# A graph-attention walk over sorted edges: the exponent's bound moved into the target table, and a quarter of each step's product moved from VectorE to ScalarE

## The reference

```python
feat = (h @ W).reshape(N, H, D)
el = einsum('nhd,hd->nh', feat, attn_l); er = einsum('nhd,hd->nh', feat, attn_r)
e = leaky_relu(el[src] + er[dst], 0.2)
emax = segment_max(e, dst); ex = exp(e - emax[dst])
denom = segment_sum(ex, dst); alpha = ex / denom[dst]
rst = segment_sum(feat[src] * alpha[..., None], dst)
out = h + elu(rst + bias)
```

## Time and profile before

| | us |
|---|---|
| median of 3 runs | 1996.78 (1994.44 to 1999.62) |
| the profiled execution, its own time | 1998.07 |
| its span from first to last instruction | 1996.4 |
| DVE busy in the span | 1503.7 (75%), 4295 instructions |
| POOL busy | 1325.6 (66%), 1235 instructions |
| PE busy | 1659.0 (83%) |
| ACT busy | 854.8 (43%) |

### The profile page before, as it was taken

The page is one execution under the profiler, slowest core; times in us unless marked ns, Lnnn a source line. Parts: engine busy times, 40 slices in busy tenths (PEclk is TensorE's granted clock), DMA queues, the critical chain, the costliest instruction groups (busy, mean ns, idle before and its releaser), DMA issues.

```text
span 1996.4 us, 48372 instructions
## 1 busy us (share of the span) xinstructions
PE 1659.0 (83%) x11492; PEld 1334.3 (67%) x11493; DVE 1503.7 (75%) x4295; ACT 854.8 (43%) x2066; POOL 1325.6 (66%) x1235
## 2 busy tenths in 40 slices
PE   7767777777787788888887675947999999999996
PEld 5545455555556677666765454936888998988885
DVE  6667677878777888888889888988666666666663
ACT  4633344444433444444444443583444434344442
POOL 2077777777777777677767774404777777777774
PEclk8979999999999999999999988557999999999998
DMA  7745556565534554444444553851333333333342
GB/s 218 231 122 144 161 148 172 151 175 159 135 110 113 141 141 128 132 138 135 127 119 131 155 193 106 301 196 35 54 51 46 51 47 52 49 47 51 46 51 28
DMA packets 150531, 238.93 MB, mean 120 GB/s; under 512 B 27984, under 2 KB 116168, under 8 KB 149192
## 3 DMA queue, kind: packets, MB, share of 16 engines
q0 software_dynamic: 62784, 134.26, 30.2%
q1 hardware_dynamic: 85944, 103.15, 15.6%
q10 hardware_dynamic: 1744, 0.85, 0.2%
HBM read 181.73 MB, written 56.44 MB: 119 GB/s over the span
## 4 chain that ended last, share of the span: by engine, by line
PE 31%; issue 19%; DVE 18%; POOL 18%; DVEq 6%; DMA 6%; POOLq 1%; ACT 0%; SPq 0%; ACTq 0%
POOL w_s L805 16%; PE bank L2233 13%; PE bank L2253 13%; DVE w_s L1501 5%; DMA w_s<-table,w_s 3%; DVEq L1436 3%; DMA out<-mid_g,acc 2%; PE bank L2219 1%; DVE w_s L1491 1%; PE bank L2046 1%; DVE w_s L1487 1%; DVE w_s L1484 1%; DMA w_s<-in_x 1%; DVE acc L1512 1%; DVE acc L1664 1%
## 5 line engine op out<-in xcount | busy, mean ns | idle before, releaser
L805 POOL DMA_INDIRECT w_s<-table,w_s x784 | 840.3, 1072 | 281.8 <-issue 235.3
L2046 PE MATMUL bank<-w_s 128*128 128x260 f32 x1952 | 513.3, 409 | 93.7 <-DVE w_s L1501 91.9
L2046 PEld LDWEIGHTS bank<-w_s 128*128 128x128 f32 x1952 | 375.0, 199 | 194.5 <-DVE w_s L1501 118.7
L1501 DVE SCALAR_TENSOR_TENSOR w_s<-w_s 128x256 f32<-128x256 f32 x976 | 347.7, 417 | 0.0
L1001 ACT COPY w_s<-bank 128x512 bf16<-128x512 bf16 x244 | 143.6, 588 | 409.0 <-PE bank L2026 314.3
L2233 PE MATMUL bank<-acc,w_s 128*128 128x256 f16 x2688 | 303.8, 273 | 0.0
L2253 PE MATMUL bank<-w_s,acc 128*128 x2688 | 302.6, 273 | 1.0 <-DVE acc L1914 1.0
L2253 PEld LDWEIGHTS bank<-w_s,acc 128*128 128x128 f16 x2688 | 262.7, 98 | 32.0 <-issue 1.3
L2233 PEld LDWEIGHTS bank<-acc,w_s 128*128 x2688 | 263.4, 98 | 30.8 <-issue 0.2
L862 POOL DMA_INDIRECT out<-mid_g,acc x112 | 196.4, 1753 | 80.7 <-POOL acc L857 47.0
L1468 DVE SCALAR_TENSOR_TENSOR w_s<-w_s,iota 128x512 bf16<-128x512 f32 x244 | 182.9, 749 | 6.7 <-issue 1.4
(11 more groups left out here) (301 smaller groups left out, 2226.5 us busy)
## 6 DMA issues: line engine op xcount, KB each, us to landing
stage<-in_L_ffn_W SPq DMA_DIRECT2D x32, 512.0 KB, 3.3
w_s<-table,w_s POOLq DMA_INDIRECT x784
w_s<-in_x SPq DMA_DIRECT2D x48, 256.0 KB, 4.2
w_s<-xT_d SPq DMA_DIRECT2D x96, 128.0 KB
w_park<-low_g SPq DMA_DIRECT2D x18, 512.0 KB
w_s<-w_park SPq DMA_DIRECT2D x9, 1024.0 KB, 9.2
xn_d<-acc SPq DMA_DIRECT2D x7, 896.0 KB, 4.7
table<-w_s SPq DMA_DIRECT2D x24, 260.0 KB, 3.6
```

Of the source, the lines that this page charges most:

```text
L805: pool.indirect_dma_start(out=ring[:, u, k, :], out_offset=None, in_=table[:, :], in_offset=bass.IndirectOffsetOnAxis(ap=ids[:, h, at + u, ...
L1501: last = dve.scalar_tensor_tensor(m[:, e:e + GH, 0:GD], rows[:, e:e + GH, 0:GD], 1.0, m[:, e:e + GH, GD:HC].to_broadcast([P, GH, GD]), ALU ...
L2046: last = pe.matmul(bank[2 + k.at % 2][:, 0:ROW], hot32[:, k.at % 4, s, :], msg[:, k.at % 2, s, :], start=s == 0, stop=s == SUB - 1)
```

## The change

It has two parts.

1. The number to subtract is stored in the table without a cap: `cap` is the leaky ReLU of the largest el of all heads (one number), and `most` in the table becomes most - cap. In the step, n = 3 becomes (most + cap) - logit, and the exponential is taken with a scale of -1. The minimum with 0 (n = 4) goes. Counts on `logit_turn` go from 5 to 4 a step. `goal` has two buffers. Three small DVE operations are added ahead of the walk.
2. The product of the last lot of 128 edges of each step is made by ACT, behind the exponential: four activations of 128x64 (one per head) with function Copy and the weight as a per-partition scale. DVE makes three pieces, and waits ahead of the third for ACT's (`part_ready`). ACT loads one register value per slot for it.

Two waits are also merged: the loads of the router's weights count on `mix_in` (9 loads in place of 7), and those who waited for 7 wait for 9.

```diff
@@ act_slot, act_weight
                 if (j + 1).live():
-                    act_weight(j + 1)
+                    slot = act.value_load(walk_i[0:1, bass.ds(j.n + 4, 1), 3:4].rearrange("p a b -> p (a b)"), min_val=0, max_val=RING - 1)
+                    act_weight(j + 1, slot)
...
-            def act_weight(k):
-                act.wait_ge(logit_turn, 5 * k.n + 5)
+            def act_weight(k, slot):
+                act.wait_ge(logit_turn, 4 * k.n + 4)
                 if k.past(2):
                     act.wait_ge(sum_ready, k.n - 1)
-                act.activation(weights(k), logit[:, k.at % 2, :, :].rearrange("p s h -> p (s h)"), ACT.Exp).then_inc(weight_ready, 1)
+                act.activation(weights(k), logit[:, k.at % 2, :, :].rearrange("p s h -> p (s h)"), ACT.Exp,
+                               scale=-1.0).then_inc(weight_ready, 1)
+                act.wait_ge(weight_ready, k.n + 1)
+                m, rows = heads_at(msg[:, k.at % 2, :, :]), ring_heads(slot)
+                for e in range((SUB - 1) * GH, SUB * GH):
+                    last = act.activation(m[:, e, 0:GD], rows[:, e, 0:GD], ACT.Copy, scale=m[:, e, GD:HC])
+                last.then_inc(part_ready, 1)
@@ DVE, ahead of the walk
+            cap = spread[:, 1:2]
...
                     lambda: dve.scalar_tensor_tensor(most, most, SLOPE, most, ALU.mult, ALU.max),
+                    lambda: dve.tensor_reduce(cap, top_n[:, 0:GH], AX.X, ALU.max),
+                    lambda: dve.scalar_tensor_tensor(cap, cap, SLOPE, cap, ALU.mult, ALU.max),
+                    lambda: dve.tensor_scalar(most, most, cap, None, ALU.subtract),
@@ dve_slot
                 if scores:
                     dve_logit(j + 1, group1, slot1, 3)
-                    dve_logit(j + 1, group1, slot1, 4)
@@ dve_logit
-                elif n == 3:
-                    last = dve.scalar_tensor_tensor(lg, lg, 1.0, most, ALU.mult, ALU.subtract)
                 else:
-                    last = dve.scalar_tensor_tensor(lg, lg, 0.0, lg, ALU.min, ALU.min)
+                    last = dve.scalar_tensor_tensor(lg, most, cap, lg, ALU.add, ALU.subtract)
@@ dve_msg
-                for e in range(0, SUB * GH, GH):
+                for e in range(0, (SUB - 1) * GH, GH):
+                    if e == (SUB - 2) * GH:
+                        dve.wait_ge(part_ready, k.n + 1)
                     last = dve.scalar_tensor_tensor(m[:, e:e + GH, 0:GD], rows[:, e:e + GH, 0:GD], 1.0,
                                                     m[:, e:e + GH, GD:HC].to_broadcast([P, GH, GD]), ALU.mult, ALU.mult)
@@ POOL ahead of the walk; PE ahead of the first keys
-            pool.wait_ge(mix_in, 7 * 16)
+            pool.wait_ge(mix_in, 9 * 16)
@@ PE ahead of the walk
-            pe.wait_ge(top_turn, 15)
+            pe.wait_ge(top_turn, 18)
```

More of the change, by code:

```diff
@@ L262, in build @@
         ids = walk([P, 2, LIST * RING, SUB], I32)
-        goal = walk([P, SUB, 2 * GH])
+        goal = walk([P, 2, SUB, 2 * GH])
         iota_i = walk([P, 256], I32)
@@ L465, in build @@
         target_ready, logit_turn, weight_ready = sem("target_ready"), sem("logit_turn"), sem("weight_ready")
-        msg_ready, sum_ready, acc_done = sem("msg_ready"), sem("sum_ready"), sem("acc_done")
+        msg_ready, part_ready, sum_ready, acc_done = sem("msg_ready"), sem("part_ready"), sem("sum_ready"), sem("acc_done")
         xa_in, kv_made, keys_ready, k_parts, keys_mapped, kv_summed = (
@@ L475, in build @@
         base_read, mid_out = sem("base_read"), sem("mid_out")
-        route_in, blank_turn = sem("route_in"), sem("blank_turn")
+        blank_turn = sem("blank_turn")
         park_in, park_high, park_low, park_out = sem("park_in"), sem("park_high"), sem("park_low"), sem("park_out")
@@ L572, in load_mix @@
                 elif n == 7:
-                    sp.dma_start(wr_s[:, :, :], wr.rearrange("(k p) n -> p k n", p=P)).then_inc(route_in, 16)
+                    sp.dma_start(wr_s[:, :, :], wr.rearrange("(k p) n -> p k n", p=P)).then_inc(mix_in, 16)
                 else:
-                    sp.dma_start(br_b[:, :], br.rearrange("(a n) -> a n", a=1).to_broadcast([P, X])).then_inc(route_in, 16)
+                    sp.dma_start(br_b[:, :], br.rearrange("(a n) -> a n", a=1).to_broadcast([P, X])).then_inc(mix_in, 16)
             load_x(0, 0)
@@ L1477, in dve_logit @@
                 lg = logit[:, k.at % 2, :, :]
-                own, most = goal[:, :, 0:GH], goal[:, :, GH:2 * GH]
+                own, most = goal[:, k.at % 2, :, 0:GH], goal[:, k.at % 2, :, GH:2 * GH]
                 if n == 0:
@@ L1481, in dve_logit @@
                 else:
-                    dve.wait_ge(logit_turn, 5 * k.n + n)
+                    dve.wait_ge(logit_turn, 4 * k.n + n)
                 if n == 0:
-                    last = dve.tensor_reduce(goal[:, :, :], at_target.rearrange("p s (c k) -> p s k c", c=3), AX.X, ALU.add)
+                    last = dve.tensor_reduce(goal[:, k.at % 2, :, :], at_target.rearrange("p s (c k) -> p s k c", c=3), AX.X, ALU.add)
                 elif n == 1:
@@ L2033, in pe_target @@
                 if k.past(1):
-                    pe.wait_ge(logit_turn, 5 * k.n - 4)
+                    pe.wait_ge(logit_turn, 4 * k.n - 3)
                 for s in range(SUB):
@@ L2129, in keys_hook @@
                     if not later:
-                        pe.wait_ge(mix_in, 7 * 16)
+                        pe.wait_ge(mix_in, 9 * 16)
                     pe_keys(first)
@@ L2166, in _ @@
             walk_turns(pe, pe_slot, keys_hook, keys_hook, queries_hook, None, pe_sum)
-            pe.wait_ge(route_in, 32)
+            pe.wait_ge(mix_in, 9 * 16)
             pe.wait_ge(v_kept, T)
```

## The result

The changed kernel takes 1961.4 us (median of 4 runs, 1960.4 to 1964.4) against 1996.7 before; the ratio is 0.9825, with a 95% interval of 0.9808 to 0.9842. The forecast was 1957, with 1935 to 1984 around it. The sum came out nearly right, but that is partly luck: two of its terms are far off and cancel, as the profile shows.

The account below looks back on a forecast made before the run. POOL was taken to bound the walk up to 650 us, DVE after. Waits 24, stretching 15 and shorter last slots 1 make 40 us off 1998.07, so 1958, or 1957 us as median of runs; range 1935 to 1984.

Parts of the forecast that it names:

- the waits: In the walk behind 650 us, POOL's waits for DVE's product to free a slot shrink, giving 24 us.
- the stretching: POOL's gathers are held by DVE's two-SBUF-input product; one piece fewer gives 15 us, also before 650 us.
- signs of being wrong: ACT's products take 0.5 us or more, DVE's slot shrinks under 0.25 us with POOL waiting, or mean gather doesn't move.
- DVE together: 650 to 1050 us: DVE saves 1.7 of 17.9 us a turn, needing 362 us against POOL's 377, so POOL bounds.
- the new wait of DVE: DVE's wait for ACT ahead of the third piece costs 0, with 1 us to spare in the shortest slots.
- Rival C: The third piece waits for ACT, 0.2 to 0.4 us a slot; only part of the stretching is left: 1988 us, chance 0.12.
- occupancy estimate: Over the walk, gathers held at a random moment by 976 product pieces of 0.417 us lose 59 us in all.
- three pieces instead of four take a quarter off: In DVE's product, the missing piece removes a quarter of the 59 us of gather stretching: 15 us, bounds 0 to 45.
- rival B: Stretching falls by 45 of 59 us, since most held gathers wait for the fourth piece: 1927 to 1940 us, chance 0.13.
- Rival A: The stretching of POOL's gathers stays, held by something else; gain 25 us, time 1972 us, chance 0.20.
- n = 4 and the fourth piece: In DVE's slot, the minimum gives 0.84 us a turn; the moved piece 0.73, limited by the register load before n = 3.
- rival D: ACT becomes the engine bounding a turn, its products taking 0.75 us each: slower, 2050 us, chance 0.05.

Follow-up runs that it names:

- experiment 5: The whole change, but DVE no longer waits for ACT's product; PE's sum and POOL's slot wait for it themselves: 1948.8 us, ratio 0.9776 to the kernel before.
- `cap_only`: The kernel before with the cap in the table and no minimum, DVE keeping all four pieces: 1982.4 us, ratio 0.9954 to the kernel before.
- the filler pair: The whole change plus one useless DVE operation where the fourth piece stood: 1981.9 us with two SBUF inputs, 1969.5 us with one.
- experiment 6: The whole change, with DVE's register load moved from between product and n = 3 to behind n = 0, into second registers: 1963.0 us, ratio 0.9850.
- experiment 1: The same run as `cap_only`: the change without ACT's part, against the kernel before: 1982.4 us, ratio 0.9954.
- experiment 8: The whole change, with PE and POOL instead of DVE waiting for ACT's product, and DVE's register load split in two: 1949.1 us, ratio 0.9776.

## Why the prediction was right, and where it wasn't

*The total* was right partly by luck. By POOL's account, the waits were to give 24 us and gave 4, the stretching 15 and gave 32. One of the forecast's own signs of being wrong came true: DVE's slot became 0.1 us shorter (17.9 to 17.5 us a turn, four slots), which is less than 0.25, and POOL still waits. Of its other signs, DVE's wait for gathered rows in the query stage, the chain going over to POOL and the absence of a wait on ACT failed too; the load ahead of n = 3 and the unchanged stages behind the walk held (774.7 and 774.3 us from the last gather to the end).

*What bounds the walk* was read rightly: POOL up to 650 us (11 to 15 us came back there, as one cuts, and by POOL's account they are stretching), DVE after.

*The waits, 24 us.* This term failed; 4 us came back (27.7 to 23.8). By the table the query turns became 12 us shorter, where the term had 21 us for that stretch. Its step was "DVE together": 16.2 us a turn for DVE, 377 us of 400 for POOL, so POOL is the bound. Both numbers may hold as loads of single engines. What neither shows is a ring over three of them. The step "the new wait of DVE, cost 0, with 1 us to spare" is the one that broke. It was worked out for the slots in which ACT has nothing beside, with the exponential starting 0.2 us after n = 3. Rival C names the other case in half a sentence, slots in which ACT has query work; there the exponential starts late, and the third piece waits 0.34 us once a turn. Over the 23 turns of this stretch the stalls by themselves are 7.4 us, but experiment 5 prices the wait at 1.0 us a turn and 10 to 13 us in all, since it also uncovers the load behind it. Even then 28.1 us of waits stay, of 31.0, so the step from POOL's higher load to vanishing waits is not borne out either: a shorter turn comes out of shorter gathers as well as shorter waits. Only `cap_only` brought the waits near nothing. Rival C had foreseen the stall and wrongly let most of the stretching stay as well.

*The stretching, 15 us.* The mechanism was right and the size was too small: 32 us, of which the filler pair confirms 18 for a piece's worth of two-input time. The occupancy estimate itself was good: counted by the DVE instruction 0.13 us after each gather's start, the product held gathers for 59.6 us before, where the estimate had 59. The step that failed is "three pieces instead of four take a quarter off". The same count gives 30.8 us after, half and not three quarters; the other operations account for the remaining 3 us. Before, 57 gathers were held on through a further piece, which alone made 20.8 us; after, it is 9 gathers and 5.7 us. That is 15 of the 29 us. It is rival B's mechanism, but B had 45 us for it. Rival A (no change) fell: of two fillers of nearly one length, the one with two SBUF inputs stretches the gathers. This agrees with the first statement of the Trainium skill ("SBUF — State Buffer", Who interferes with whom), that such an operation contends with a GpSimd instruction that reads SBUF. By the inference there, that such an operation doesn't stall a DMA's descriptor generation, the gathers would not have been stretched, and they were. Whether what is held is that step or the gather's reading of its ids, which lie in SBUF, was not shown.

*n = 4 and the fourth piece.* As forecast, the load limits the slot: the issue time ahead of n = 3 went from 46.1 / 244 = 0.19 us on average (0.24 in the slot of rows 8) to 107.7 / 244 = 0.44. n = 3 itself went from 0.18 to 0.24 us with its scalar from memory, within the 0.07 allowed.

*ACT's product.* 337 ns each and 1.06 us for four, against 0.27 and 1.1: starts are 0.24 us apart, so the sum was right though the single duration was short. The Trainium skill ("ScalarE: Activation LUTs", What ACT_TABLE_LOAD costs) gives 280 ns + 0.833 ns a column with a pointer operand and an overlap of 93 ns; for 64 columns that makes, as an estimate, 333 ns each and 240 ns from start to start. The trace agrees: the median is 333 ns, and 0.24 us lie between two starts.

*The rest.* The operations ahead of the walk and the merged loads cost nothing that can be seen: the first gather starts at 98.3 us, as before at 98.5. Two numbers of the working have no source: no row shows the 0.12 us a turn for DVE's sequencer, and rival D's 2050 should be 2057 by its own terms (1997 + 60). Neither decides anything here.

## What to carry to other kernels

When an engine's load drops below its neighbour's, ask what cross-engine ring remains before crediting the difference: follow the one slot of a turn in which the helper engine is busiest, not the average slot. A new wait should stand where nothing slow is queued behind it, or with whoever really needs the data; here moving it from DVE to PE and POOL was worth more than a quarter of the whole change. And count what an offloaded operation frees besides its own time: moving ACT's part alone took 22.5 us of stretching off POOL's gathers and 8 us off its waits for DVE. Shorter gathers were worth time where POOL was the bound (10 of the 12 us between the two fillers), and none in the query turns.

## What the runs showed of the hardware that was not expected

- A gather on POOL takes its 949 ns or is held by a DVE operation with two SBUF inputs: fillers of 418 ns (two inputs) and 410 ns (one) gave 832 and 814 us for the same 784 gathers. In the trace after the change nearly every held gather (263 of 269 with such an operation running at its start) lasts, to 20 ns, until that operation ends, plus 0.82 us. Of 335 gathers that had no such operation at their start and one that began within 0.9 us behind it, none was held. In the trace before, 57 gathers were held on through a further piece of the product that followed without a pause.
- A register load of five words at a stride of 20 bytes takes 1183 ns in the median and about 590 in every fourth row; four words aligned to 16 bytes take 344 and one takes 317. It stops the sequencer of its engine, whoever needs the values (1.88 us of issue time ahead of the one-hot in experiment 6).
- Shortening DVE's slot can lengthen the gathers: from 840 us before to 850 in experiment 1, and from 795 in experiment 5 to 805 in experiment 8.
